# Turning softmax probabilities by transposes in the first layer, and a later fetch in the third cross attention

## What is computed

```
q        = layer_norm(x) Wq                      # 56 x 128
scores   = q (ctx Wk)^T * scale                  # 56 x 1500
probs    = softmax(scores)                       # over the 1500 rows
evidence = probs (ctx Wv)                        # = (probs ctx) Wv
```

## Time and profile before

| | us |
|---|---|
| median of 3 runs | 1776.51 |
| lowest and highest | 1770.99, 1777.41 |
| the profiled execution, its own time | 1769.27 |
| its span, first to last instruction | 1767.5 |
| PE, DVE, ACT, POOL busy | 1562.3, 1164.7, 976.2, 659.8 |
| mean granted clock of TensorE | 0.919 of full speed |

### The profile page before, as it was taken

One profiled execution on the slowest core, in us unless ns is written; L12 is line 12 of the kernel. 1 busy time (PEld: TensorE's weight loads), 2 busy tenths in 40 slices (PEclk: granted clock), 3 DMA queues, 4 the chain that ended last, 5 costly groups with the idle time before them and its releaser, 6 DMA issues.

```text
span 1767.5 us, 49986 instructions
## 1 busy us (share of the span) xinstructions
PE 1562.3 (88%) x20479; PEld 996.4 (56%) x20479; DVE 1164.7 (66%) x2425; ACT 976.2 (55%) x1878; POOL 659.8 (37%) x898
## 2 busy tenths in 40 slices
PE   7999977499999998887999999988887999899886
PEld 5667733166666665543566666655443566566554
DVE  3555455577777777366777777764557777777572
ACT  2333323077777677332567776764332677676663
POOL 4000074146666643446366665610332222222110
PEclk9889889599999999798799999997897999999897
DMA  8444214145665544024355655432033466666520
GB/s 240 125 138 145 84 45 95 40 120 133 159 164 152 133 110 116 1 71 109 82 143 152 161 148 147 116 94 47 1 71 93 120 150 160 156 155 146 124 62 6
DMA packets 193275, 199.49 MB, mean 113 GB/s; under 512 B 58949, under 2 KB 182536, under 8 KB 193048
## 3 DMA queue, kind: packets, MB, share of 16 engines
q1 hardware_dynamic: 191464, 195.22, 43.6%
q10 hardware_dynamic: 1008, 1.05, 0.2%
q0 software_dynamic: 576, 0.02, 0.0%
HBM read 114.46 MB, written 72.17 MB: 106 GB/s over the span
## 4 chain that ended last, share of the span: by engine, by line
PE 69%; DVE 13%; ACT 11%; issue 4%; DMA 2%; POOL 1%; SPq 1%; DVEq 0%; ACTq 0%; POOLq 0%
PE PS L1414 14%; PE PS L1242 9%; PE PS L1440 8%; PE PS L1235 7%; PE PS L1388 5%; DVE mx L1881 4%; ACT q_parts L1009 3%; PE PS L1178 3%; PE PS L1188 3%; PE PS L1516 3%; PE PS L1195 3%; ACT v_sb L918 2%; PE PS L1229 2%; PE PS L1089 2%; PE PS L1426 2%
## 5 line engine op out<-in xcount | busy, mean ns | idle before, releaser
L1881 DVE TENSOR_REDUCE mx<-PS 112x1 f32<-112x500 f32 x1152 | 713.5, 672 | 213.3 <-PE PS L1388 211.3
L1009 ACT ACTIVATE q_parts<-PS 125x448 f32<-125x448 f32 x1152 | 562.0, 543 | 159.3 <-PE PS L1440 151.5
L741 POOL CAST k_hi<-k_full 128x500 f16<-128x500 f32 x144 | 89.0, 618 | 631.3 <-issue 556.7
L1440 PEld LDWEIGHTS PS<-q_st,k_st 50*125 50x125 f16 x4608 | 183.5, 137 | 232.1 <-ACT q_parts L1009 162.6
L776 POOL TENSOR_SCALAR cx<-cx,norm_b 125x128 f32<-125x128 f32 x384 | 306.7, 814 | 19.8 <-issue 15.9
L1440 PE MATMUL PS<-q_st,k_st 50*125 50x112 f16 x4608 | 258.7, 233 | 41.5 <-ACT q_parts L1009 32.3
L1414 PE MATMUL PS<-q_parts,v_sb 125*18 125x112 f32 x9216 | 289.0, 268 | 0.0
L1414 PEld LDWEIGHTS PS<-q_parts,v_sb 125*18 125x18 f32 x9216 | 216.3, 100 | 53.2 <-issue 41.3
L1388 PE MATMUL PS<-k_st,q_mx 50*112 50x500 f16 x1080 | 225.2, 384 | 7.6 <-DVE mx L1881 5.2
L743 POOL TENSOR_TENSOR k_lo<-k_full,k_hi 128x500 f16<-128x500 f32 x144 | 163.8, 1138 | 21.1 <-POOL k_hi L741 3.6
L918 ACT ACTIVATE v_sb<-PS 125x512 f32<-125x512 f32 x144 | 86.8, 603 | 98.3 <-PE PS L1242 98.3
(11 more groups left out here) (283 smaller groups left out, 2087.2 us busy)
## 6 DMA issues: line engine op xcount, KB each, us to landing
k_st<-k_dram SPq DMA_DIRECT2D x288, 187.5 KB, 3.6
k_dram<-k_hi SPq DMA_DIRECT2D x288, 125.0 KB, 3.0
cx<-in_ctx SPq DMA_DIRECT2D x40, 672.0 KB
k_dram<-k_lo SPq DMA_DIRECT2D x144, 125.0 KB, 3.1
xT_dram<-k_full SPq DMA_DIRECT2D x16, 750.0 KB, 4.9
cx<-xT_dram SPq DMA_DIRECT2D x32, 375.0 KB
v_sb<-in_ctx SPq DMA_DIRECT2D x8, 672.0 KB
q_st<-q_all SPq DMA_DIRECT2D x48, 99.8 KB
```

Of the source, the lines that this page charges most:

```text
L1009: act.activation(probs[:, c % RING, u * HR:(u + 1) * HR], PS[0:KC, (2 * c + u) % SC_RING, 0:HR], ACT.Exp).then_inc(sem("exp_done"), 1)
L1440: last = mm(PS[0:KC, (2 * c + a) % SC_RING, k * PW:k * PW + PW], k_st[64 * a:64 * a + ROWS, p, k, c * KC:(c + 1) * KC], q_st[64 * a:64 * a ...
L1881: dve.tensor_reduce(mx[:, r, t:t + 1], PS[0:PW, MX_BANK + u % MX_RING, 0:TK], AX.X, ALU.max)\
```

## The change

Five edits belong together, in the first layer. `turn_probs` transposes the blocks of probabilities instead of multiplying them with the diagonal, and no longer waits for it. `l0_evidence` swaps its operands: the turned probabilities are the weights (56 columns) and the context chunk moves (128 columns), so that the evidence comes out by rows, 56x128. DVE's `scale_evidence(b-1)`, in the place of `reciprocal_diagonal(b)`, waits for that evidence and multiplies its rows with the reciprocals into `ev_rows`. PE's `turn_evidence(b-1)`, behind `turn_ctx(b+1)`, transposes the scaled rows, in one instruction, into the bank they came from. ACT's `copy_evidence(b-1)` waits for that and stands behind `copy_ctx(b+1)`.

The sixth edit is in SP's list for the third cross attention: the fetch of batch b+3 moves from ahead of the key writes and reads of b+2 to behind them.

```diff
--- before.py
+++ after.py
@@ -324,7 +324,7 @@
         p0 = A_first[0:T, :, :].rearrange("p k r -> p (k r)")[:, 0:2 * S].rearrange("p (a s) -> p a s", a=2)
         pT0 = probs[0:KC, 0, 0:C * T]
         max3 = sb("max3", [T, 2, NT])
-        diag0 = sb("diag0", [T, 2, T])
+        ev_rows = sb("ev_rows", [T, 2, D])
         neg0 = sb("neg0", [T, 2])
         sum0 = sb("sum0", [T, 2])
         rec0 = sb("rec0", [T, 2])
@@ -656,13 +656,13 @@
                         q_max(behind)
                         if layer < 3 and b + 4 < B:
                             load((b + 4, i + 2, p))
-                        if layer == 3 and b + 3 < B:
-                            load((b + 3, (b + 3) // 2, 1 - p))
                         k_out(behind, 0)
                         k_in(behind, 0)
                         k_out(behind, 1)
                         k_in(behind, 1)
                         k_out(behind, 2)
+                    if layer == 3 and b + 3 < B:
+                        load((b + 3, (b + 3) // 2, 1 - p))
                     if b == SPLIT_BATCH:
                         q_out(1)
                     if b == SPLIT_BATCH + 1:
@@ -873,16 +873,16 @@
                                bias=neg0[:, p:p + 1], accum_out=sum0[:, p:p + 1]).then_inc(sem("p0_done"), 1)
 
             def copy_evidence(b):
-                act.wait_ge(sem("ev_ready"), b + 1)
+                act.wait_ge(sem("evT_ready"), b + 1)
                 act.activation(rows_of(A[6], b), PS[:, NT * (b % 2), 0:T], ACT.Copy).then_inc(sem("evT_done"), 1)
 
             copy_ctx(0)
             for b in range(B):
                 l0_exp(b)
+                if b + 1 < B:
+                    copy_ctx(b + 1)
                 if b:
                     copy_evidence(b - 1)
-                if b + 1 < B:
-                    copy_ctx(b + 1)
                 copy_probs(b)
             copy_evidence(B - 1)
 
@@ -1181,20 +1181,24 @@
             def turn_probs(b):
                 p = b % 2
                 pe.wait_ge(sem("p0_done"), b + 1)
-                pe.wait_ge(sem("diag0_done"), b + 1)
                 for u in range(2):
                     for c in range(6):
                         k = 6 * u + c
-                        last = mm(PS[0:KC, 3 * p + 1 + u, c * T:(c + 1) * T], p0[:, p, k * KC:(k + 1) * KC], diag0[:, p, :],
-                                  start=True, stop=True)
+                        last = pe.transpose(PS[0:KC, 3 * p + 1 + u, c * T:(c + 1) * T], p0[:, p, k * KC:(k + 1) * KC],
+                                            ident[0:T, 0:T])
                     last.then_inc(sem("p0T_ready"), 1)
 
             def l0_evidence(b):
                 pe.wait_ge(sem("p0T_done"), 2 * (b + 1))
                 for c in range(C):
-                    last = mm(PS[:, NT * (b % 2), 0:T], cx0[b % 4][:, c, :], pT0[:, c * T:(c + 1) * T],
+                    last = mm(PS[0:T, 3 * (b % 2), 0:D], pT0[:, c * T:(c + 1) * T], cx0[b % 4][:, c, :],
                               start=(c == 0), stop=(c == C - 1))
                 last.then_inc(sem("ev_ready"), 1)
+
+            def turn_evidence(b):
+                p = b % 2
+                pe.wait_ge(sem("ev_done"), b + 1)
+                pe.transpose(PS[:, 3 * p, 0:T], ev_rows[:, p, :], ident[0:T, 0:T]).then_inc(sem("evT_ready"), 1)
 
             def preparation(layer):
 
@@ -1253,10 +1257,13 @@
                     l0_evidence(b - 1)
                 if b + 1 < B:
                     turn_ctx(b + 1)
+                if b:
+                    turn_evidence(b - 1)
                 turn_probs(b)
                 if b + 1 < B:
                     l0_scores(b + 1)
             l0_evidence(B - 1)
+            turn_evidence(B - 1)
             pe.wait_ge(sem("w_loaded"), 16 * (len(WEIGHTS) - len(FIRST_WEIGHTS) + 2 * E))
             pe.wait_ge(sem("cxT0_done"), NT * B)
             by_anchor = [w1[:, k // 2, 2, (k % 2) * D:(k % 2 + 1) * D] for k in range(2 * E)]
@@ -1693,13 +1700,14 @@
                 dve.tensor_copy(mean_all[:, b, :], aggr[:, :, 0]).then_inc(sem("stats_mean"), 1)
                 dve.tensor_copy(var_all[:, b, :], aggr[:, :, 1]).then_inc(sem("stats_done"), 1)
 
-            def reciprocal_diagonal(b):
+            def scale_evidence(b):
                 p = b % 2
                 dve.wait_ge(sem("p0_done"), b + 1)
                 dve.reciprocal(rec0[:, p:p + 1], sum0[:, p:p + 1]).then_inc(sem("rec0_done"), 1)
+                dve.wait_ge(sem("ev_ready"), b + 1)
                 dve.wait_ge(sem("rec0_done"), b + 1)
-                dve.tensor_scalar(diag0[:, p, :], ident[0:T, 0:T], rec0[:, p:p + 1], None, ALU.mult)\
-                   .then_inc(sem("diag0_done"), 1)
+                dve.tensor_scalar(ev_rows[:, p, :], PS[0:T, 3 * p, 0:D], rec0[:, p:p + 1], None, ALU.mult)\
+                   .then_inc(sem("ev_done"), 1)
 
             row_stats(0, range(C))
             for b in range(B):
@@ -1709,10 +1717,10 @@
                     keep_stats(0)
                 else:
                     row_stats(b, range(5))
-                reciprocal_diagonal(b)
-                if b:
+                    scale_evidence(b - 1)
                     row_stats(b, range(5, C))
                     keep_stats(b)
+            scale_evidence(B - 1)
 
             dve.wait_ge(sem("anchors_ready"), 1)
             e1 = place["L0_xcond_e_b1"]
```

## The result

| | before | after |
|---|---|---|
| median, us (runs) | 1776.96 (4) | 1754.93 (4) |
| lowest and highest | 1770.99, 1781.99 | 1751.61, 1755.92 |
| the profiled execution, its own time | 1769.27 | 1754.28 |
| its span | 1767.5 | 1752.5 |

The ratio is 0.9866, with a 95% interval of 0.9832 to 0.9899: faster by 22 us, where 49.5 were forecast. Between the two profiled executions it is 15.0 us where 44.5 were forecast, and these 29.5 missing ones are what has to be found.

The account below looks back on a forecast made before the run. PE, busy 88% of the span, was taken as the bound. First layer 43.5 us plus third cross attention 1 us made 44.5 off 1769.3, so 1724.8; the median was forecast at 1727, range 1708 to 1746.

Parts of the forecast that it names:

- The third cross attention: Fetch of batch b+3 moved behind key writes and reads: 1 us won in all (5 won to 4 lost).
- I take the early end, because the key writes no longer stand behind the fetch.: Third cross attention: fetch landing taken at 1485.6, of 1485.6 to 1489.8, before the key product's use at 1488.90.
- up to 1 us: Third cross attention: possible loss in most bodies from the moved fetch, the first above all.
- Rival 4: Third cross attention: fetch late in each body, some 2 us in 13 bodies, 1752 us; chance 0.04.
- The waits for key data ... one of 2.1 us: Third cross attention: this present wait, followed by a short clock fall, could be won, 2 to 5 us.
- The transposes' price: First layer: 12 transposes of probabilities in 0.7 us at full clock, 1.3 at low; bounds 0.65 and 1.35.
- rival 5: First layer: transposes cost as products, scores at 142.15, 6 us less won, 1733; chance 0.74 together with the forecast.
- That also makes the transposes' exact price nearly idle: First layer: scores wait for ACT's evidence copy until 141.7; at the transposes' upper bound they start at 142.15.
- The clock: First layer: 11 of the 11.8 us of low-clock excess won, since the sparse stretch shrinks and evidence moves more columns.
- First batch: First layer's first batch, at low clock: 5 us won (3.5 to 6), 3.9 from transposes replacing products.
- Last batches: End of the first layer: 1.7 won, 0.9 lost, 2 for clock and what follows; together 3 us (0 to 6).
- The evidence by rows and its scaling: First layer: evidence products unchanged at 2.75 us for 24, DVE scaling 0.3 us, the round trip costing nothing.

Follow-up runs that it names:

- rows_with_products: The changed kernel with the fetch in its old place and 24 products with the identity instead of the 12 transposes; 1785.36 us (one run).
- plain_transposes_56_moving: The kernel before with plain transposes for the diagonal products, evidence as it was, scaling by row sums left out; 1741.93 us (one run).
- blocks_of_128: The changed kernel with the fetch in its old place, probabilities in blocks of 128 columns, 125 filled, all 128 loaded; 1735.2 us, ratio 0.9766.
- fetch_between: The changed kernel with the fetch between the first key read and the second key write; 1745.36 us, ratio 0.984.

## Why the prediction was wrong

The sum missed 29.5 us of the profiled execution: 18 in the third cross attention, 8.6 in the first layer, the other 2.9 behind and between them.

- **The third cross attention** is the step that failed: "I take the early end, because the key writes no longer stand behind the fetch." The bounds had been worked out (landing at 1485.6 to 1489.8 for a use at 1488.90), and the choice between them was wrong three times over. The fetch went out 14.8 to 18.4 us behind the body's first key product, where the forecast had 13.5 to 17.7 (1479.7 and 1483.9 less 1466.19) and took the early end; the landing took 5.9 to 8.1 us at the waits, not 5.9. The use was read from one body of before, 22.7 us long (1466.19 to 1488.90), while before also has three bodies of 20.7 us, and after waits at the end of all three. And a lateness was priced at "up to 1 us" per body, though the five waits took 1.5 to 4.7 us each and the fetch now closes a loop, in which a late key product makes the next fetch late too. Behind some of the waits the clock falls as well (2.00 us at batch 8 for a product of 1.11). Rival 4 named it ("late in each body") and had 0.04; its time, 1752, is 3 us from the result. Its price of 26 us was partly that of the third cross attention (17 us), partly by chance that of the transposes.
- "The waits for key data ... one of 2.1 us": that one did go, as said; after has none at the maxima. A wait of 2.1 us was traded for 12.9.
- **The transposes' price** is a term that was mis-sized: 12 in 1.47 us (1.40 to the next product), where 0.7 was taken from a row of 112 columns. The upper bound, 1.35, was the right number, and with it the scores' start at 142.15 in the old timeline. This is rival 5, "the transposes cost as products", record for record; it was priced at 6 us and cost 6.3. "That also makes the transposes' exact price nearly idle" fell with it: the cycle saved 1.30, not 1.75, so 14 cycles gave 18.2 instead of 24.5. The trace of before could not settle it. It has the weight load of this very operand, but in a product (L1188's, durations as above), and products of 128 columns load as slowly (189 ns), while its transposes, of 112 and 128 columns, load in 131 and 141 ns; none has 125:

```profile
L1188 PEld LDWEIGHTS PS<-diag,A_first x384: 180/186/329, 39.0 to 206.8; 56*125 56x125 f32 x192
```

- **The clock** was right: all of the 11.8 us (11 taken) came back, 151.5 - 121.55 = 30.0 = 18.2 + 11.8. The reason given, that the sparse stretch is shorter, fits rows_with_products, where it isn't shorter and the clock falls, but isn't separated there from the change of record. The one beside it, that the evidence moves more columns, doesn't hold for the cycles, since plain_transposes_56_moving holds the clock without it.
- **First batch** 2.4 us instead of 5: at low clock the transposes took 2.77 us, not 1.3 (the scores got back 1.2 of their 5.25, as supposed), and this batch began 1.4 us later. **Last batches** 2.5 instead of 3.
- **The evidence by rows and its scaling** cost what was said: 2.72 us for 24 to the next instruction (2.75 was taken) and a DVE instruction of 0.34 (0.3), hidden behind the context's transposes.
- With the transposes at the price that was forecast, the first layer also gives what was forecast: blocks_of_128 has a cycle of 8.12 us (8.2) and a lead of 45.3 (43.5).

## What to carry to other kernels

Before a transfer is moved behind others in a queue, follow its use back to the issue: if the chain leads through the same queue into the previous body, the transfer closes a loop, and what counts is whether the loop is shorter than the shortest body, not whether the landing is in time in one body of today's timeline. The place that gave the shortest traces with the whole fetch here was behind a write and in front of the read that waits for that write's landing; in front of a write the fetch made that write land late. And a price for an operation is taken from a row with the same operation in the same shape. Where there is none, as here, the bound from the dearer neighbour (1.35 us) belongs in the sum until a run has measured it.

## What the hardware showed that was not expected

- In a transpose, a weight load of 125 fp32 columns on 56 rows takes 186 ns, one of 124 columns 136 and one of 128 columns 139 ns; 12 transposes take 1.47, 0.88 and 0.91 us. Loading three columns more is faster. In products 125 and 128 columns take the same (188 and 189 ns). Whether it is the odd number of columns or something else in 125 wasn't tried.
- Transposes, one behind another, did not pull the granted clock down in 14 cycles, and 24 products of the same 56 columns in their place did; in the profiles that was worth 11.8 us, beside 18.2 for the shorter cycle itself.
- Two transfers of 375 KB each took 5.9 to 8.1 us from issue to landing while the keys' writes and reads were under way, against 4.9 for one of 750 KB, a write, in the first layer. In its turn the fetch delays a key write right behind it, which took 4.4 to 6.2 us to its read in fetch_between.
